# Moving VectorE's last weight pieces and the first tiles' scales behind the last batch's norms in a fused attention and mixture-of-experts kernel

## The reference, cut to what matters

```python
x = x + tanh(g_xattn) * attention(layernorm(x), ctx)   # 8 batches of 256 rows, 16 heads, 120 context rows
x = x + tanh(g_ffn) * moe(layernorm(x))                # 8 experts, each row goes to its best 2

q = x @ w_q;  k, v = context @ w_kv
attn = softmax(q @ k.T / 8);  out = (attn @ v) @ w_out + b_out
probs = softmax(x @ Wr.T);  the two best experts of a row, their weights made to sum to 1
h = silu(x @ W1[e].T);  y = h @ W2[e].T;  out = sum over the two experts of gate * y
```

## Time and profile before

| what | value |
|---|---|
| median of 3 runs | 532.32 us (531.59 to 533.25) |
| the profiled execution: its own time | 530.12 us |
| its span, from the first to the last instruction | 528.4 us |
| busy TensorE / VectorE / ScalarE / GpSimd | 482.2 / 364.0 / 371.4 / 369.7 us |
| TensorE's granted clock, mean over the span | 0.982 of full |

### The profile page before, as it was taken

How to read it: one execution, slowest core, us unless ns; L and a number is a source line. 1 busy time by engine, 2 the same in 40 slices (tenths; PEclk the granted TensorE clock), 3 DMA queues, 4 the chain that set the end, 5 groups by cost and what they waited for, 6 DMA issues and landing times. The chain is left out here.

```text
span 528.4 us, 17570 instructions
## 1 busy us (share of the span) xinstructions
PE 482.2 (91%) x6630; PEld 431.7 (82%) x6630; DVE 364.0 (69%) x866; ACT 371.4 (70%) x577; POOL 369.7 (70%) x414
## 2 busy tenths in 40 slices
PE   2889699999999999999776999898999999999994
PEld 2877578888897888888556899888999999999993
DVE  5799899899989989898996757544344443444431
ACT  1888989999899998988764577544555655546551
POOL 5469779798999999899988566546554645545432
PEclk9999989999999999999897999999999999999998
DMA  7953415163261626335174648877888888888712
GB/s 288 398 197 117 146 55 188 51 208 117 91 223 46 229 63 192 115 105 198 39 252 142 211 126 293 253 198 210 257 223 251 235 232 263 218 244 245 211 23 30
DMA packets 35060, 94.86 MB, mean 180 GB/s; under 512 B 4507, under 2 KB 24475, under 8 KB 27645
## 3 DMA queue, kind: packets, MB, share of 16 engines
q1 hardware_dynamic: 25812, 82.79, 45.7%
q0 software_dynamic: 8592, 10.81, 11.4%
q10 hardware_dynamic: 576, 0.14, 0.1%
HBM read 74.45 MB, written 19.28 MB: 177 GB/s over the span
## 5 line engine op out<-in xcount | busy, mean ns | idle before, releaser
L1541 DVE SCALAR_TENSOR_TENSOR hT<-hf,h_scale,hT 128x512 f16<-128x512 f32 x78 | 58.3, 750 | 86.1 <-ACT hT L1016 86.1
L1707 PE MATMUL st_bank<-xsT,w_tile 128*128 128x128 f16 x1872 | 113.9, 222 | 1.3 <-DVE xsT L1535 1.3
L1707 PEld LDWEIGHTS st_bank<-xsT,w_tile 128*128 128x128 f16 x1872 | 110.1, 99 | 2.1 <-DVE xsT L1535 1.6
L730 POOL DMA_INDIRECT out<-yt,row_of x39 | 62.4, 1600 | 61.8 <-DVE yt L1550 49.0
L1010 ACT ACTIVATE hf<-st_bank,z_scale 128x512 f32<-128x512 f32 x78 | 52.9, 678 | 44.6 <-PE st_bank L1707 38.6
L618 POOL TENSOR_TENSOR pT<-pT 120x512 f16<-120x512 f32 x64 | 77.3, 1223 | 6.1 <-ACT pT L884 5.9
L1707 PE MATMUL o_bank<-w2s,hT 128*128 x600 | 69.7, 273 | 0.3 <-DVE yt L1550 0.3
L1016 ACT ACTIVATE hT<-hf,h_scale 128x512 f16<-128x512 f32 x78 | 56.3, 722 | 10.6 <-PE o_bank L1707 4.3
L1707 PEld LDWEIGHTS o_bank<-w2s,hT 128*128 128x128 f16 x600 | 57.4, 98 | 7.3 <-issue 0.8
L883 ACT ACTIVATE pT<-st_bank,exp_bias,logit_scale 120x512 f32<-120x512 f32 x64 | 50.0, 781 | 14.9 <-PE st_bank L1924 14.4
L663 POOL TENSOR_SCALAR stage<-stage,upw 128x512 f32<-128x512 f32 x32 | 56.6, 1769 | 4.1 <-ACT w_hi L983 4.1
(11 more groups left out here) (224 smaller groups left out, 1008.3 us busy)
## 6 DMA issues: line engine op xcount, KB each, us to landing
w_tile<-w_split SPq DMA_DIRECT2D x39, 1024.0 KB, 5.9
stage<-in_w SPq DMA_DIRECT2D x16, 1024.0 KB, 5.0
w_split<-w_hi SPq DMA_DIRECT2D x8, 512.0 KB, 2.8
w_split<-stage SPq DMA_DIRECT2D x8, 512.0 KB, 3.9
out<-x SPq DMA_DIRECT2D x17, 128.0 KB
xin<-in_x SPq DMA_DIRECT2D x8, 256.0 KB
w2s<-in_wkv SPq DMA_DIRECT2D x2, 1024.0 KB, 12.0
xres<-in_x SPq DMA_DIRECT2D x16, 128.0 KB, 2.1
```

Of the source, the lines that this page charges most:

```text
L730: pool.indirect_dma_start(out=out[0:rows], out_offset=bass.IndirectOffsetOnAxis(row_of[:, t:t + 1], 0), in_=yt[t % XG][:], in_offset=None, ...
L1541: nc.vector.scalar_tensor_tensor(out=hT[par][:, 1, 4 * a:4 * a + 4, :], in0=hf[par][:, 512 * a:512 * a + 512].rearrange("p (c n) -> p c n" ...
L1707: ins = pe.matmul(out, lhs[i](a), rhs[i](c), start=(i == 0 and a + c == 0), stop=(i == n - 1 and a == 1))
```

## The change

On VectorE the last expert's two quarters of the down weights' low part (`split_low(7, 1, 1)` and `(7, 1, 0)`) no longer stand before the norms of batch 7's unit 0, half 1, but in front of `norm_o(7, 3, 0)`. The three stages of the early tiles' scales and their gates leave the front part of step p = 7 and stand behind `norm_o(7, 1, 1)`, `norm_o(7, 2, 0)` and `h_split` of tile 0. ScalarE no longer waits for the gates: the semaphore, renamed to `units_done`, is raised when `h_scale` is written. On GpSimd the last `p_low(7, 2, 1)` stands ahead of the scatters of batch 5 and the last expert's quarters 2 and 3 move from there to behind `p_low(7, 3, 1)`. On TensorE the transposed scores of batch 7's last unit, `col_scores(7, 3)`, stand one product earlier.

```diff
@@ GpSimd
-                p_low(p + 6, 2, 1)
+                p_low(p + 6 if p != 1 else B, 2, 1)
                 scatter(p + 4, 1)
                 norm2_factors(p + 5)
                 p_low(p + 6, 3, 0)
                 tile_add(p + 4, 2)
                 p_low(p + 6, 3, 1)
+                split_low(E - 1 if p == 1 else E, 1, 2)
+                split_low(E - 1 if p == 1 else E, 1, 3)
...
                 p_low(p + 7, 2, 0)
-                split_low(E - 1 if p == 0 else E, 1, 2)
-                split_low(E - 1 if p == 0 else E, 1, 3)
+                p_low(B - 1 if p == 0 else B, 2, 1)
                 tile_gather(p + 5, 8)
                 scatter(p + 5, 0)
@@ ScalarE
-                act.wait_ge(tables_done, 1 if isinstance(t, int) and t < EARLY else 2)
+                act.wait_ge(units_done, 1 if isinstance(t, int) and t < EARLY else 2)
@@ VectorE, the end of by_tile for h_scale
+                ins = nc.vector.tensor_reduce(dst, by_expert[:, 0:n], AX.X, ALU.add)
+                if late is None:
+                    chain.link(ins)
+                else:
+                    ins.then_inc(units_done, 1)
+                    dve.wait_ge(units_done, 1 + late)
...
-                nc.vector.tensor_tensor(gate_y[:, c], gate_y[:, c], y_scale[:, c], ALU.mult).then_inc(tables_done, 1)
+                chain.link(nc.vector.tensor_tensor(gate_y[:, c], gate_y[:, c], y_scale[:, c], ALU.mult))
@@ VectorE, the list
-                tile_scales(p, 0, 0)
...
-                tile_scales(p, 0, 1)
...
-                tile_scales(p, 0, 2)
...
-                tile_gates(p, 0)
...
+                tile_scales(p, 0, 0)
                 tile_low(p, 0)
                 score_scale(p + 2)
                 norm_o(p, 2, 0)
                 row_max(p + 1, 2)
+                tile_scales(p, 0, 1)
                 tile_low(p, 1)
...
                 tile_h_low(p, 0, 0)
+                tile_scales(p, 0, 2)
+                tile_gates(p, 0)
+                split_low(E - 1 if p == B - 1 else E, 1, 1)
+                split_low(E - 1 if p == B - 1 else E, 1, 0)
                 norm_o(p, 3, 0)
...
-                split_low(p + 1, 1, 1)
+                split_low(p + 1 if p + 1 < E - 1 else E, 1, 1)
...
-                split_low(p + 1, 1, 0)
+                split_low(p + 1 if p + 1 < E - 1 else E, 1, 0)
@@ TensorE, the list
                 out_product(p, 1, 1)
+                col_scores(B - 1 if p == B - 2 else B, 3)
                 x_T(p + 3)
...
-                col_scores(p + 1, 3)
+                col_scores(p + 1 if p != B - 2 else B, 3)
```

More of the change, by code:

```diff
@@ L369, in build @@
         experts_done = sem("experts_done")
-        tables_done = sem("tables_done")
+        units_done = sem("units_done")
         rows_done = sem("rows_done")
@@ L1484, in add_turns, with by_tile @@
                                                op0=ALU.mult, op1=ALU.add).then_inc(turns_done, 1)
-            def by_tile(vec, dst, n):
+            def by_tile(vec, dst, n, late=None):
                 chain.link(nc.vector.tensor_tensor(by_expert[:, 0:n], one_hot[:, 0:n], vec.unsqueeze(1).to_broadcast([P, n, E]),
                                                    ALU.mult))
-                chain.link(nc.vector.tensor_reduce(dst, by_expert[:, 0:n], AX.X, ALU.add))
+                ins = nc.vector.tensor_reduce(dst, by_expert[:, 0:n], AX.X, ALU.add)
[4 more added lines that the diff above has]
+                    dve.wait_ge(units_done, 1 + late)
             def tile_scales(b, late, stage):
@@ L1512, in up_scales @@
                 by_tile(z8, z_scale[:, c], c.stop - c.start)
-                by_tile(h8, h_scale[:, c], c.stop - c.start)
+                by_tile(h8, h_scale[:, c], c.stop - c.start, late)
             def down_scales(late):
```

## The result

| | kernel before | changed kernel |
|---|---|---|
| median | 531.16 us (527.89 to 533.99, 22 runs) | 532.79 us (530.43 to 537.6, 22 runs) |
| ratio, 95% interval | | 1.004 [1.0021, 1.0058] |
| profiled execution: time, span, mean granted clock | 530.12, 528.4, 0.982 | 531.67, 529.9, 0.986 |

The change costs 0.4%, 2.1 us. I had forecast 1.9 us gained.

What follows compares the result with a forecast made beforehand. TensorE, 91% busy, was taken as the bound, its idle time lying at 260 to 300 us. A 2.7 us head start less 0.8 for the clock gives 1.9 us gained: 530.4 us from a 532.32 median, range 528.0 to 533.5.

Steps and rivals of the forecast that it cites:

- What was taken away in front: VectorE's front norms, rid of split and scales: values(7, 2, 0) 6 us sooner, up_half(0, 0) 4.2 us sooner.
- What was put in behind: Scales, gates and two splits on VectorE ahead of norm_o(7, 3, 0): 2.8 us taken as likely, 2.2 to 9.3 possible.
- The head start at `norm_o(7, 3, 0)`: This VectorE norm of batch 7 starts 1.5 to 4.0 us sooner than 293.80; 2.7 us taken.
- the second fall of the clock: TensorE's clock falling again at the wait ahead of values(7, 3, 1): costs 0 to 2.5 us, 0.8 taken.
- Given back: Third rival, 0.23: wait moves to norm_o(7, 3, 0), clock falls a second time; 531.6 to 533.9 us.
- the new wait of some 2.5 us: TensorE's wait ahead of values(7, 3, 1), grown from 0.45 us; said to be alone and shorter than 2.80.
- The credit at tile 0: Part of the half-clock loss at tile 0 is saved: 2.7 us head start, half of the stretch at half clock.
- Off the path, at no cost: GpSimd's moved splits, the gates' semaphore and transfers cost nothing; a 4.96 us GpSimd wait covers the 2.7 us head start.
- the wait for tile 9's rows growing instead of moving: Sign of a wrong prediction: TensorE's wait ahead of tile 9 gets longer; no size given.
- The scores: Moving col_scores(7, 3) one product earlier on TensorE is alone worth nothing.
- The semaphore and GpSimd's splits: The gates' semaphore costs nothing either way; GpSimd's two moved splits, ending near 290.4, leave its gathers about where they were.
- Slower: Rival, 0.16: VectorE's splits at the new places starve behind GpSimd's low parts, 2.75 us lost each; 534 to 537 us.

Runs made afterwards that it cites:

- e8: Changed kernel with VectorE's two splits put back to their old places ahead of the norms of unit 1; ratio 1.0011 to the kernel before.
- e9: Changed kernel with VectorE's two splits alone moved behind norm_o(7, 3, 1), scales and gates staying ahead of norm_o(7, 3, 0); ratio 0.9987 to the kernel before.
- e10: e5 plus 30 idle matmuls on TensorE ahead of tile 9's transposes; ratio 0.9924 to the kernel before.
- e2: Changed kernel with 50 idle matmuls on TensorE ahead of values(7, 3, 1); ratio 0.9967 to the kernel before.
- e3: Changed kernel with 30 idle matmuls on TensorE ahead of tile 9's transposes; ratio 1.0028 to the kernel before.
- e4: Changed kernel with both sets of idle matmuls, ahead of values(7, 3, 1) and of tile 9's transposes; ratio 1.0001 to the kernel before.
- e7: Changed kernel with TensorE's order as before, col_scores(7, 3) back behind values(7, 1, 1); ratio 1.0043 to the kernel before.
- e5: Changed kernel with third-stage scales, gates and VectorE's two splits moved behind unit 3's norms, plus 14 idle matmuls ahead of values(7, 3, 1); ratio 0.9917 to the kernel before.
- e11: Kernel before with 30 idle matmuls on TensorE ahead of tile 9's transposes; ratio 1.002 to the kernel before.
- e1: Changed kernel with the third stage of the scales, the gates and VectorE's two splits moved behind the norms of unit 3; ratio 0.9961 to the kernel before.

## Why the prediction was wrong

**What was taken away in front: right.** The 3.50 us split is gone. Measured from `ranks(5)`, `values(7, 1, 0)` comes 1.5 us sooner, `values(7, 2, 0)` 5.8 us (predicted 6) and `up_half(0, 0)` 4.6 us (predicted 4.2). A detail was wrong: the last to come for it were ScalarE's exponentials, not VectorE's low part.

**What was put in behind: right in size.** Predicted 2.8 us; the rows from 287.79 to 290.95 make 3.16 us. The two splits cost 1.41 of it, less than the 2.1 I had given them, and the small product of the scales 1.22 instead of 0.26: the product of GpSimd's own split beside it was stretched too, to 1.55 us (1.16 in e8). By the Trainium skill ("SBUF — State Buffer", section "Who interferes with whom") an instruction of VectorE with two inputs in SBUF contends with one of GpSimd that reads SBUF, and the ports that they share are "an exclusive lock". The product of the scales fits a wait for one such instruction: it ran 0.96 us longer than alone, beside one product of GpSimd. The 3.50 and 3.51 us of the split in front do not, since they went on past the first of GpSimd's. e9 and e10 give the price in arrivals: `values(7, 3, 1)` at 20.15, without the splits at 18.84, without the scales and gates either at 17.16, all three with the clock up at tile 0.

**The head start at `norm_o(7, 3, 0)`: right.** Predicted 2.7 us, 1.5 with the clock down at tile 0 and 4.0 with it up; the norm starts at 290.95 instead of 293.80, 2.85 us sooner, and 4.0 us sooner measured from `ranks(5)`, with the clock up. With the clock down (e2, e3, e4) it is 2.25 us by the first leg.

**The step that failed is the price of the second fall of the clock: "I take 0.8".** It measured 2.3 and 2.9 us in the two profiles of the changed kernel, at or over the upper bound of 2.5 that I had given it. With that wait filled the leg is 4.18 (e2) and 4.17 us (e4) again, and the ratio 0.9967 and 1.0001 instead of 1.004. Two judgements led to 0.8. The wait was put at "about 2.5" us, but the prediction's own terms, 0.45 us of wait that was there and 2.8 us of work put in, make 3.25; measured, 0.45 and 3.16 make 3.61. TensorE's pace at tile 0 does not enter: e3 waited 3.69 us there and e7 3.92 with tile 0 slowed by the clock. And I held against the rival *Given back* that "the new wait of some 2.5 us is one alone and shorter than 2.80". The runs bear out no such comfort: in all seven profiles in which TensorE stood at this norm for 0.89 us or more with nothing to fill it (0.89 to 3.92 us), the clock fell behind it. A wait priced as likely to bring the clock down, at the 2.5 us of the old stretch, would have left 2.7 - 2.5 = 0.2 us of gain instead of 1.9, no change that the runs can tell.

**The credit at tile 0 can't be checked by the mean.** The head start counts on part of the clock's fall at tile 0 being saved. Before's one profile lost 528.4 x 0.018 = 9.5 us to the clock, its 89 executions 6.2 in the mean, and only 8 of them have a clock of 0.982 or lower. So by its clock that profile is near the low end. But its excess need not lie at tile 0: it has falls at 64 and 252 us too, 1.7 us each, which the changed kernel's first profile has not. How often each kernel loses at tile 0, and how much, stays open. What is shown is the sum of all places: at a full clock the change gains 1.9 ± 0.9 us, under the 2.7 of the head start, and it loses up to 4.4 ± 0.9 us more to the clock, where the prediction had 0.8 for the new fall. Part of those 4.4 us is time in which TensorE stood: the window from 290 to 292 us, at 0.57, counts 0.86 us as lost, with TensorE busy for 0.27 us of it.

**"Off the path, at no cost": incomplete.** The scatter of batch 6 does come sooner, at 301.76 us, 1.7 us sooner measured from `ranks(5)`. But "the wait for tile 9's rows growing instead of moving" was my sign of a wrong prediction, and it grew, from 1.71 to 2.32 and 2.36 us, with the clock falling behind it in both profiles, 1.5 and 1.8 us. The text had named the wait and not asked what a longer one does. That this fall is part of the mean loss fits e3's lost time (9.0 against 10.5); but its ratio can't be told from the changed kernel's, the same fall is missing behind e5's 2.35 us, and before shows an equal one later with its wait filled (e11). How much of the 2.1 us it is stays open.

**The scores: right** (e7). The semaphore and GpSimd's splits were also put at no cost; they were not run apart, so that is not shown.

Of the rivals the third, *Given back*, is the one that came in by its mechanism: a wait moved to `norm_o(7, 3, 0)`, and a second fall. Its range of times has a slip: 532.3 us and 1.0 lost make 533.3, not 533.9. *Slower*, by starved splits, did not come in: the two splits took 1.41 us together (2.31 in e7's profile, the longest).

## What to carry to other kernels

Where work is moved in front of an instruction that TensorE waits for, add the whole of it to the wait that is already there (here 0.45 + 3.16 = 3.61 us), and then ask what that wait does to the clock: the fall behind it can cost about as much again (2.3 and 2.9 us in the leg behind it). Here it was the same 3 us of small work a few instructions later that made the difference between 1.004 and 0.9961. And before the clock of one profile is taken as the baseline, look at the mean granted clock of all executions: span times clock and the remainder split a result into work and clock, though not by place. A single profile shows the places, but not how often.

## What the runs showed of the hardware

- Idle matmuls in a wait can be worth more than the wait: 50 of them in a wait that stayed (2.96 us, with 0.90 us still idle behind them) took the work behind it from 6.48 and 7.10 us to 4.18. In e5, 14 of them (0.94 us) took it from e1's 5.82 us to 4.17. The Trainium skill ("TensorE: Matmul & The Clock Gate", section "HAM oscillation — how this bites in real kernels") reckons the cost of a low clock as half of the time spent at it; here the windows from 292 to 298 us lose 1.0 + 1.0 + 0.54 = 2.5 us, and the leg 2.3.
- They don't save it for certain: with tile 9's wait filled, e11's clock fell 16 us later behind a wait of 1.40 us, where before had stood 1.33 us with the clock up.
- The length of one wait does not decide alone. Behind 1.91 us at tile 9 the clock fell (e9), behind 2.35 us it did not (e5).
- An instruction of VectorE over 104 elements, 0.26 us long, took 1.22 us beside GpSimd's `tensor_tensor`, and the gates' of 13 elements 1.74 us in the earlier trace rows, but 0.25 in its new place in the changed kernel's profile and 1.09 in the same place in those of e2, e3 and e4.
